# Another order of TensorE's blocks and ScalarE's readings in the attention turns, and a prologue in which VectorE turns only batch 0

## What is computed

```python
# attention: 8 heads of 16 channels, 512 queries by 512 keys, for each of 16 batches
q = _apply_rotary(q_emb, split_heads(_proj(layernorm(x), Wq, bq)))
k = _apply_rotary(k_emb, split_heads(_proj(c, Wk, bk)))
v = split_heads(_proj(c, Wv, bv))
# _apply_rotary: t * cos(pos) + rot(t) * sin(pos), rot swaps the halves of a head, one with its sign changed
p_attn = softmax(einsum('bhtc,bhsc->bhts', q, k) / sqrt(16))
x = x + _proj(einsum('bhts,bhsc->bhtc', p_attn, v), Wo, bo)
# experts: router, top 8 of 32, silu(g) * u, down projection, weighted sum
x = x + ffn(layernorm(x))
```

## Time and profile before

| | us |
|---|---|
| median of 3 runs | 1097.98 |
| lowest and highest | 1095.36, 1100.32 |
| the profiled execution | 1095.91 |
| its span in the profile | 1094.1 |

### The profile page before, as it was taken

How to read it: one execution, slowest core, us unless ns; L and a number is a source line. 1 busy time by engine, 2 the same in 40 slices (tenths; PEclk the granted TensorE clock), 3 DMA queues, 4 the chain that set the end, 5 groups by cost and what they waited for, 6 DMA issues and landing times.

```text
span 1094.1 us, 29937 instructions
## 1 busy us (share of the span) xinstructions
PE 1002.8 (92%) x7276; PEld 482.4 (44%) x7277; DVE 710.7 (65%) x1365; ACT 772.1 (71%) x1797; POOL 734.9 (67%) x667
## 2 busy tenths in 40 slices
PE   6589999999999999992599999999999999999996
PEld 2122222222222222231366556666666666666663
DVE  6878899999999988886353555454554554454521
ACT  2278888888888887771367667767677766777674
POOL 3034577777777775457467777877777777777775
PEclk9599999999999999996699999999999999999999
DMA  6324444444444434320588789888789898898674
GB/s 206 108 82 123 139 129 129 128 128 122 127 126 124 119 103 122 99 87 22 177 224 211 210 202 235 227 212 213 206 200 235 221 222 202 224 214 213 118 141 90
DMA packets 89267, 175.60 MB, mean 160 GB/s; under 512 B 23818, under 2 KB 40762, under 8 KB 85106
## 3 DMA queue, kind: packets, MB, share of 16 engines
q0 software_dynamic: 38464, 75.58, 32.6%
q1 hardware_dynamic: 50736, 99.26, 28.1%
q10 hardware_dynamic: 4, 0.02, 0.0%
HBM read 118.30 MB, written 61.58 MB: 164 GB/s over the span
## 4 chain that ended last, share of the span: by engine, by line
PE 41%; issue 3%; DVEq 3%; DVE 2%; DMA 1%; ACTq 1%; ACT 1%; POOL 0%; POOLq 0%; SPq 0%
PE ps L1843 22%; PE ps L1851 5%; PE ps L1869 2%; PE ps L1873 2%; PE ps L1871 2%; PE ps L1870 2%; PE ps L1872 2%; DVEq L366 2%; DVE w_lo L1439 1%; PE ps L1859 1%; DVE w_hi L1434 1%; ACTq L366 1%; PE ps L1861 1%; PE ps L1860 1%; POOL expert_rows L617 0%
## 5 line engine op out<-in xcount | busy, mean ns | idle before, releaser
L1070 DVE TENSOR_REDUCE mx<-ps 128x2 f32<-128x1024 f32 x256 | 303.8, 1221 | 32.9 <-PE ps L1815 29.7
L1843 PE MATMUL ps<-w_hi,o_raw 128*128 x1200 | 317.6, 327 | 0.0
L802 ACT ACTIVATE pr<-ps 128x512 f32<-128x512 f32 x512 | 278.6, 603 | 46.2 <-PE ps L1792 45.2
L776 POOL DMA_INDIRECT out<-v,s_idx x148 | 247.3, 1671 | 91.4 <-ACT g_idx L792 51.0
L755 POOL DMA_INDIRECT pr<-normalised_tokens,g_idx x154 | 167.1, 1085 | 53.2 <-issue 22.5
L1843 PE MATMUL ps<-w_lo,o_raw 128*128 x600 | 196.0, 327 | 0.0
L792 ACT ACTIVATE o_raw<-ps 128x1024 f16<-128x1024 f16 (+1 forms) x183 | 175.0, 956 | 1.4 <-PE ps L1851 1.2
L1451 DVE SCALAR_TENSOR_TENSOR rope_b<-rope_a,stacks,ps 128x192 f32<-128x192 f32 x150 | 61.4, 409 | 150.0 <-ACT rope_a L957 96.3
L1843 PEld LDWEIGHTS ps<-w_hi,o_raw 128*128 128x128 f16 x1200 | 117.6, 98 | 85.7 <-issue 1.2
L617 POOL DMA_INDIRECT expert_rows<-rows,rowi x128 | 128.7, 1005 | 38.3 <-issue 37.3
L1804 PE MATMUL ps<-pr,v 128*32 128x512 f32 x1024 | 136.4, 605 | 0.4 <-issue 0.3
(11 more groups left out here) (177 smaller groups left out, 1467.4 us busy)
## 6 DMA issues: line engine op xcount, KB each, us to landing
stage<-in_expert_w SPq DMA_DIRECT2D x32, 1280.0 KB
stacks<-qk_parts SPq DMA_DIRECT2D x128, 96.0 KB, 3.4
w_lo<-in_x SPq DMA_DIRECT2D x32, 256.0 KB, 2.8
w_lo<-in_ctx SPq DMA_DIRECT2D x32, 256.0 KB, 5.7
qk_parts<-qk SPq DMA_DIRECT2D x32, 256.0 KB
qk_parts<-qk SPq DMA_DIRECT2D x32, 128.0 KB
out<-x SPq DMA_DIRECT2D x16, 256.0 KB, 4.0
normalised_tokens<-x2s SPq DMA_DIRECT2D x16, 256.0 KB
```

The source lines that it names most:

```text
L776: nc.gpsimd.indirect_dma_start(out_rows, bass.IndirectOffsetOnAxis(s_idx[:, s.slot(4), 0:1], 0), y_sb[:, s.slot(4), :], None, bounds_check ...
L802: nc.scalar.activation(pr[:, n % 8, :], bank(f"s{n}"), ACT.Exp, scale=DH ** -0.5).then_inc(exp_done, 1)
L1070: V.tensor_reduce(mx[:, b.slot(2), at:at + 3:2, tile], bank(f"m{n}"), AXX, ALU.max).then_inc(mx_done, 1)
L1843: last = mm(ps[:, s.slot(2), 0:2 * INTER], xt[:, s.slot(2), at:at + P], w[:, cols], start=(m == 0), stop=(m == 3 * KT - 1))
```

## The change

In the prologue only batch 0 keeps its rotation on DVE. For batches 1 and 2 ACT reads the turned projections, and POOL multiplies, adds and makes the low halves. POOL's four start-up DMAs move from before its first normalising to behind the third. PE's prologue puts m(0) to m(3) between the projections. In DVE's turn -1 the statistics of x come behind the second maximum. In the full turn ACT's `read_o(bo, 1)` comes behind `normal_x2`, `high_of_x2` before exponential 6, `exponentials_of_top` before 28 and `high_of_qk(bq, 1)` from before 24 to before 30; PE has m(1) before the turned projection, m(2) before s(8), m(5) behind s(14), s(16) before m(7), m(8) before s(18), s(22) before m(10), the transposed maxima behind pv(5), m(13) behind s(26), and m(15) before s(30).

```diff
+    ROPES = 1
@@ gpsimd: setup
-            for r in range(4):
-                gp.dma_start(started_d[r:r + 1, :], started[:, :]).then_inc(added[r], 16)
@@ gpsimd: turn
-                if isinstance(it.k, int) and it.count(1) < 0:
-                    return
-                if isinstance(it.k, int) and it.count(1) == 0:
+                if turn_no is not None and turn_no < ROPES - FILL:
+                    return
+                if turn_no == ROPES - FILL:
+                    start_adds()
                     gp.wait_ge(turn_in, 32)
@@ scalar: prologue turns
+                    if it.count(1) == ROPES - FILL:
+                        act.wait_ge(turn_in, 32)
+                    by_act = it.count(1) >= ROPES - FILL
+                    if bq.live() and by_act:
+                        turned_half(bq, 0)
                     if bl.live():
                         normal_x()
+                    if bq.live() and by_act:
+                        turned_half(bq, 1)
@@ scalar: turn
                 exponentials(0, 6)
+                if br.live():
+                    normal_x2(br)
                 if bo.live():
                     read_o(bo, 1)
                 if br.live():
-                    normal_x2(br)
-                exponentials(6, 1)
-                if br.live():
                     high_of_x2(br)
-                exponentials(7, 1)
+                exponentials(6, 2)
...
@@ vector: prologue turns
+                if turn_no == -1:
+                    rope(bq, 0)
+                    rope(bq, 1)
+                    maxima(0, 2)
+                    stats_of_x()
+                    maxima(2, 14)
+                    return
+                stats_of_x()
                 if isinstance(it.k, int) and it.count(1) < 0:
...
+                    if it.count(1) == -FILL:
                         first_rope(bq, 0)
                         first_rope(bq, 1)
-                    if it.count(1) == -1:
-                        maxima(0, 4)
-                    if bq.live():
                         first_low(bq, 0)
                         first_low(bq, 1)
...
@@ tensor: turn
                 s(6)
+                m(1)
                 if bq.live():
                     bank_is_free(pe, it, "qr")
                     project_turned(bq, 0)
...
-                m(1)
                 pv(0)
+                m(2)
                 s(8)
-                m(2)
                 pv(1)
...
```

More of the change, by code:

```diff
@@ L604, in _, with start_adds @@
             gp.wait_ge(gp_init, 1)
-            for r in range(4):
-                gp.dma_start(started_d[r:r + 1, :], started[:, :]).then_inc(added[r], 16)
             gp.wait_ge(half_set, 1)
+            def start_adds():
+                for r in range(4):
+                    gp.dma_start(started_d[r:r + 1, :], started[:, :]).then_inc(added[r], 16)
             def scatter_rows(b, ks):
@@ L693, in turn @@
                 scatter_rows(bs, (6, 7))
-                if turn_no is not None and turn_no < FILL:
+                if turn_no is not None and 0 <= turn_no < FILL:
                     store_pads(turn_no)
@@ L1690, in turn @@
                     if b1.live():
-                        for n in range(9):
+                        for n in range(4, 9):
                             m(n)
```

49 lines of the change are left out of this document (25 added, 24 removed).

## The result

The changed kernel takes 1108.09 us (median of its five executions, 1104.9 to 1108.4), against 1097.98 before (five as well): a ratio of **1.0092** with a 95% interval of 1.0079 to 1.0105. The forecast was 1097.1 and "the same", its range ended at 1103. The kernel is slower, near the price of rival (a), 1111.

A forecast was written before the change was run, and what follows sets the result against it. No engine alone was taken as the bound, but a path that changes engine several times a turn. Full turns +0.4, turns 0 and 1 -0.3, prologue -1.0: -0.9 from 1097.98 gives 1097.1 us, range 1089.5 to 1103.

The forecast's parts named there:

- rival (a): Full turns: denominators come the full 1.77 late, output waits 1.1 us a turn, +14 us, 1111; chance 0.14.
- POOL's last low half waits 1.6 longer for ACT ... Hidden.: End of full turn: scatters and the stack's store behind the low half have time, so the delay costs nothing.
- This is the narrowest cover of the change.: Full turn's output: POOL's second product ends at 270.30, PE needs it at 270.75; hidden by 0.4 only.
- 4.37 behind: SP's queue in a full turn: den_load follows the denominators' store by 4.37, so comes at 255.88, not 254.11.
- m(1) ... a wait that isn't there today.: Full turn's start: m(1) waits for DVE's maximum of m(0) until 250.70, making pv(0) 0.25 late.
- the reciprocals come back 0.28 later: Full turn: POOL, waiting for the reciprocals, starts at 266.68 instead of 266.40; the output stays covered.
- read_o behind normal_x2: hidden: ACT in a full turn: reading ends at 251.51, pv(0) needs it at 252.02; exponential 7 is also in time.
- Turns 0 and 1: -0.3.: First two turns: m(1) doesn't wait, DVE's last maximum comes up to 0.2 earlier; -0.3 us, bounds 0 to -0.6.
- The prologue: -1.0.: Prologue ends 1.0 us earlier, DVE's first maximum at 28.0 instead of 29.46; bounds -1.7 to 0.
- Rival (c): Full clock is back before turn 0, which takes about 27.0 instead of 29.06; -3.5 us, 1094.5; chance 0.07.
- Rival (b): Full turns: waits for maxima and exponentials go, half a microsecond a turn; -7.8 us, 1090; chance 0.19.
- the step from the profiled execution to the median: Whole kernel: the median of the runs lies 2.07 above the profiled execution, taken from the kernel before.

The follow-up runs named there:

- e7: Kernel before with one edit: high_of_qk(bq, 1) late, behind the exponentials of the top, before exponential 30; ratio 1.0064 to the kernel before.
- e13: Changed kernel with the second row of maxima and den_load ahead of the stack's load on SP; 1104.4 us, ratio 1.0068 to the kernel before.
- e14: Changed kernel with den_load and second maxima row ahead of SP's stack load, and high_of_qk(bq, 1) right behind high_of_qk(bq, 0); 1096.45 us, 0.9995 to the kernel before.
- e8: Kernel before with only the new order of TensorE's blocks in the full turns; ratio 1.0059 to the kernel before.
- e6: Kernel before with only ScalarE's reading of o moved behind normal_x2; ratio 1.0098 to the kernel before.
- e16: Kernel before with the new prologue and TensorE's new order, but m(1) left behind the turned projection; ratio 0.9985 to the kernel before.
- the second group: Runs on one chip (kernel before: 1096.4 us): the changed kernel again, 1.0118, and three single edits on the kernel before, 1.0059 to 1.0098.
- e15: Kernel before with only SP's second row of maxima and den_load ahead of the stack's load; ratio 1.0001 to the kernel before.
- e3: Changed kernel with ScalarE's reading of o and high_of_qk(bq, 1) both put back early; ratio 1.0052 to the kernel before (1129.8 us).

## Why the prediction was wrong

**"POOL's last low half waits 1.6 longer for ACT ... Hidden."** This is the step that failed first. I looked for who waits for the low half (scatters, the store of the stack), found nobody, and was right in that: no row after shows such a wait. What I didn't ask is beside what it now runs. It moved from 269.98, in the kernel before, into the time of `chosen`, at 271.97 there, and this is 0.67 us a turn (e7) or 5.8 us in the changed kernel (e13 against e14). The term stood at nothing in the sum. No rival had it, and that (a) came near the measured time is luck: its price was for something else.

**"This is the narrowest cover of the change."** The way through the denominators was followed rightly in the undisturbed turn, to 0.04 us (10.60 against 10.64, 12.53 against 12.51). The step that failed is the one before: den_load was put "4.37 behind" the store "in the queue today" as if that were fixed. Single issues of SP take 0.5 to 1.6 us longer now and then. In the kernel before four of the second loads of the stack took 2.5 to 3.4 us instead of 1.76, with nothing waiting behind them. With the reading of o later, such a hold falls on the load ahead of den_load in five turns of the changed kernel. The cover in the prediction was also looked for at the far end, at GpSimd's products (0.4); the tight place was the reciprocal, where the slack was 0.4 (0.89 late, the turn 0.49 longer): the next maximum is behind it and TensorE's m(7) behind that. Price: 5.5 us by the profiles, not the 14 of rival (a), since it counts in five turns, with 0.5 to 0.9 in four of them and 3.0 in one. The output's wait for GpSimd, which (a) named as its mark, was there once, for 2.1 us.

**"m(1) ... a wait that isn't there today."** Right: m(1) comes at 255.82 in the turn from 250.36 with 0.24 for VectorE's maximum. e8 has 27.74 where 27.73 was forecast, and without the early m(1) it is 27.48: the 0.25 that m(1) costs and the 0.21 to 0.22 that the rest earns are both there. So are the steps between. In e14's turn from 243.05, m(7), m(12), pv(5) and the output stand at 14.38, 20.84, 21.16 and 25.52 after the start; forecast were 14.37, 20.84, 21.16 and 25.51 (259.61, 266.08, 266.40 and 270.75, less 245.24). Only the waits for a maximum at m(7) and m(12) aren't there any more. What failed is "the reciprocals come back 0.28 later": that took the time of their store and load as fixed, and with the new order the store lands some 2 us late in turns 10, 12 and 14. This is the third step that failed, at 3 to 5 us an execution (5.1 in e8, about 3 in e14).

**"read_o behind normal_x2: hidden"** holds for ScalarE and TensorE in the changed kernel (27.74 in e14). It isn't so with the old order of TensorE, where s(8) pays 0.22 for it (e6).

**Turns 0 and 1: -0.3.** They gave -0.99 (-0.88 and -0.11), more than the bound of -0.6. Turn 0 begins at the granted clock of 0.50, and its length goes with the moment at which the clock is back at 1.00, which the sum left out: 7.8 us into the turn before (29.06), 6.8 in the changed kernel (28.18) and 7.1 in e14 (28.22), but 8.1 in e13 (28.73) and 8.3 in e16 (28.89), which have the same prologue. So this gain isn't a firm one.

**The prologue: -1.0.** It gave -0.73 in this pair of profiles. The end of the prologue moves by itself: it is at 50.66, 50.67, 52.23, 52.26 and 52.32 in the profiles of the old prologue on the chips at 1096 to 1098, and at 48.98 to 49.93 in the five of the new one, so the size agrees no better than to a microsecond. The steps came true: the first maximum at 27.59 (28.0 forecast), VectorE's cosine product behind a wait for GpSimd's sum, and the projections among the maxima at half clock (2.07 for a pair). In the trace after:

```profile
26.92 0.75 DVE L1083 SCALAR_TENSOR_TENSOR rope_a<-ps,pb,cf 128x512 f32<-128x512 f32 x1 [1.87 <-POOL rope_s L727]
27.59 1.22 DVE L1077 TENSOR_REDUCE mx<-ps 128x2 f32<-128x1024 f32 x1
29.40 2.07 PE L1513 MATMUL ps<-xn,pw 128*128 128x512 f32 x2
```

Rival (c), the clock back before turn 0, didn't come: turn 0 still takes 28.18, and the clock is back a microsecond sooner in it. Rival (b) is half there: the stops at m(7) and m(12) that were its mark are gone, but other blocks stand in their place, and 27.48, not 27.2, is what the order can do once m(1) is put back. Its reason against was misread too: VectorE is busy for 25.43 of the 27.70, so 2.3 us of a turn are idle and not 1.3.

The sum of the prediction, with the failed steps at their measured 5.8 and 5.5 and 3 for the late rcb, is 1097.1 + 14.3 = 1111.4; the kernel took 1108.1 and, in the second group, 1110.2. About 2 of the 3.3 between lie in the step from the profiled execution to the median, which the prediction took over from the kernel before (2.07): the changed kernel's profiled execution is its median.

## What to carry to other kernels

When an instruction moves in time, ask not only who waits for it but what runs beside it on the other engine of the pair: here a VectorE operation with two SBUF inputs stood still until a GpSimd operation on SBUF was done, and the profile shows it as a longer duration (1.31 for 0.41), not as a wait. In a queue that many transfers share, put the short transfer on which a chain hangs ahead of the long ones; that cost nothing here (e15), and with it the alternation was gone from the turns (e13). And a margin of 0.4 us, worked out from one even turn, is none where single issues of that queue take up to 1.6 us longer.

## What was not expected of the hardware

- `chosen` was once held though its record starts 0.50 us ahead of GpSimd's operation (1.96 us in place of 0.41), with a transfer of expert rows running on GpSimd in between.
- The store of the reciprocals, a small DMA, lands after 2.7 to 3.7 us in place of 1.4 to 1.6 in the same three turns (10, 12 and 14) of every trace with TensorE's new order that tells the landing. Why isn't known.
- SP's issues of a DMA, 0.43 us each, take 1.0 to 2.0 now and then: about once in two turns in the kernel before (1.07 to 1.98), twice in two turns in the one after (1.23 to 1.77) and in e6 (1.20 to 1.63). The place changes with the order of the program. What holds them wasn't found.
- In the kernel after, TensorE is busy for 2.50 of the 4 us from 146 to 150, and the granted clock is 0.63 in the mean from 150 to 153. In e16 it is busy for 0.73 of the 3 us from 350 to 353, and the clock is 0.65 from there to 356.7. These two turns, of 31.40 and 31.30, have a mean clock of 0.95 and 0.96, the other turns shown here 1.00.
- The same kernel took 1096.4, 1097.4, 1098.0, 1128.0 and 1129.8 us on five occasions, and the ratio of two kernels isn't the same on a slower chip (0.9995 for e14 at 1097, 1.0052 for e3, which differs from it only in the reading of o and SP's order, at 1130).
